# New instruction orders on five engines of an attention and recurrence block, with folded means and two transfer queues

## The reference

```python
def _ln(v, eps):
    return (v - mean(v, -1)) / sqrt(var(v, -1) + eps)

y = _ln(x, 1e-6)
q, k, v = (einsum('oc,ncij->noij', M, y) for M in (Wq, Wk, Wv))
qk = einsum('ncij,nchj->nihj', q, k) / d
qrq = einsum('ncij,chi->nihj', q, rq) / d
krk = einsum('ncij,chi->nihj', k, rk) / d
weight = softmax(qk + Gq * qrq + Gk * krk, axis=3)
out = einsum('nihj,nchj->ncij', weight, Gv1 * v) + einsum('nihj,chi->ncij', weight, Gv2 * rv)
x = x + out
t = x.reshape(16, 1024, 32)
Wx = einsum('bti,hi->bth', _ln(t, 1e-5), W)
Wx = (Wx - mean) * rsqrt(var + 1e-5) * gamma + beta      # over all b, t
y_t = sigmoid(Wx_t + y_(t-1) @ V.T)                      # 1024 steps
return t + ys
```

## Time and profile before

| | us |
|---|---|
| median of 3 runs | 154.19 |
| lowest, highest | 152.92, 155.33 |
| the profiled execution | 154.99 |
| its span, first to last instruction | 153.1 |

### The profile page before, as it was taken

The page is one execution under the profiler, slowest core; times in us unless marked ns, Lnnn a source line. Parts: engine busy times, 40 slices in busy tenths (PEclk is TensorE's granted clock), DMA queues, the critical chain, the costliest instruction groups (busy, mean ns, idle before and its releaser), DMA issues.

```text
span 153.1 us, 4782 instructions
## 1 busy us (share of the span) xinstructions
PE 101.6 (66%) x2063; PEld 70.5 (46%) x2064; DVE 96.2 (63%) x158; ACT 73.6 (48%) x161; POOL 61.9 (40%) x62
## 2 busy tenths in 40 slices
PE   0769978686598880999755950358208987999400
PEld 0313312475588770888655950112002336999400
DVE  5996874000304879705501896379988969888992
ACT  8957786347700236692230030332343449999500
POOL 8995439840000687740500054555343000003940
PEclk9999999999779999599999999557965999999965
DMA  4880899899000002434332000000000000000467
GB/s 138 294 206 0 189 206 237 192 226 188 12 4 4 4 4 54 106 75 101 91 90 58 4 4 0 2 0 0 0 0 0 4 0 0 0 6 0 144 197 208
DMA packets 9825, 11.67 MB, mean 76 GB/s; under 512 B 2828, under 2 KB 6924, under 8 KB 9804
## 3 DMA queue, kind: packets, MB, share of 16 engines
q1 hardware_dynamic: 9612, 10.84, 28.0%
q10 hardware_dynamic: 192, 0.52, 1.4%
HBM read 2.97 MB, written 2.10 MB: 33 GB/s over the span
## 4 chain that ended last, share of the span: by engine, by line
DVE 27%; PE 18%; SPq 15%; ACT 13%; issue 11%; DMA 8%; POOL 5%; POOLq 0%; ACTq 0%
SPq L286 7%; PE ps L1033 5%; PE ps L990 5%; ACT warm L658 4%; DMA gates<-in_L_conv_Gk_dram 4%; SPq L291 4%; DVE xin L351 3%; DMA v_tile<-u_tile 3%; PE ps L1043 3%; DVE stat L786 3%; DVE y_tile L357 3%; DVE u_tile L782 2%; DVE rel_tile L816 2%; PE ps L1020 2%; ACT v_tile L658 2%
## 5 line engine op out<-in xcount | busy, mean ns | idle before, releaser
L1054 PE MATMUL ps<-rel_tile,w_bd 128*128 128x512 f32 x16 | 12.6, 888 | 10.9 <-DVE rel_tile L816 10.9
L357 POOL TENSOR_TENSOR y_tile<-xin,u_tile 128x256 f32<-128x256 f32 (+1 forms) x7 | 7.1, 1049 | 23.6 <-DVE xin L351 23.6
L990 PE MATMUL ps<-spread,v_tile 128*32 128x64 f32 x512 | 13.5, 269 | 4.4 <-DMA v_tile<-u_tile 3.0
L407 POOL TENSOR_TENSOR att_tile<-att_tile,soft 128x1024 f32<-128x1024 f32 x4 | 7.8, 1946 | 19.1 <-DVE soft L746 19.1
L990 PEld LDWEIGHTS ps<-spread,v_tile 128*32 128x32 f32 x512 | 12.6, 195 | 5.4 <-issue 4.5
L757 DVE TENSOR_TENSOR u_tile<-ps,xin 128x512 f32<-128x512 f32 x8 | 5.5, 684 | 15.0 <-PE ps L1033 15.0
L596 ACT ACTIVATE square<-y_tile 128x512 f32<-128x512 f32 x8 | 4.9, 629 | 18.4 <-POOL y_tile L428 18.4
L428 POOL TENSOR_TENSOR y_tile<-u_tile,stat 128x512 f32<-128x512 f32 x7 | 7.3, 1048 | 15.6 <-DVE stat L788 15.6
L1043 PE MATMUL ps<-spread,v_tile 128*32 128x64 f32 x512 | 9.2, 223 | 6.4 <-issue 6.4
L887 DVE TENSOR_SCALAR ps<-att_tile,bnv 128x512 f32<-128x512 f32 (+1 forms) x18 | 12.3, 762 | 1.2 <-ACT warm L658 1.1
L1020 PE MATMUL ps<-w_bd,y_tile 128*32 128x128 f32 x256 | 9.2, 307 | 5.0 <-ACT v_tile L510 5.0
(11 more groups left out here) (103 smaller groups left out, 234.1 us busy)
## 6 DMA issues: line engine op xcount, KB each, us to landing
spread<-rel_tile SPq DMA_DIRECT2D x32, 64.0 KB, 2.0
out_dram<-y_tile SPq DMA_DIRECT2D x8, 256.0 KB, 2.3
xin<-in_x_dram SPq DMA_DIRECT2D x3, 512.0 KB, 4.9
spread<-att_tile SPq DMA_DIRECT2D x12, 128.0 KB, 3.5
v_tile<-u_tile SPq DMA_DIRECT2D x12, 128.0 KB, 3.1
xin<-in_x_dram SPq DMA_DIRECT2D x2, 256.0 KB, 2.8
spread<-u_tile SPq DMA_DIRECT2D x4, 128.0 KB, 2.3
att_tile<-in_L_conv_rv_dram SPq DMA_DIRECT2D x4, 128.0 KB, 2.7
```

Of the source, the lines that this page charges most:

```text
L357: return eng.tensor_tensor(result[:, :, rows, :], back[:, at:at + P * k].rearrange("p (q i j) -> p q i j", q=Q, i=k), x2[:, :, rows, :], A ...
L407: nc.gpsimd.tensor_tensor(att_m[:, n, :, :], att_m[:, n, :, :], soft[:, 0, n, :].unsqueeze(2).broadcast_to([P, C, C]), ALU.subtract).then_ ...
L990: return nc.tensor.matmul(ps[group(g), first + j // 8, at:at + Q * HALF].rearrange("p (q i) -> p q i", q=Q), u_by_q[:, g, :, j], y_bd[:, : ...
L1054: nc.tensor.matmul(bank(WX_BANK[k % 2]), w_bd[:, 1, :], by_row(tokens, k), start=True, stop=True).then_inc(S["wx_product"], 1)
```

## The change

It moves instructions in the lists of all engines, and does some of them in another way:

- VectorE's mean of a row is gone as an instruction. Where VectorE centres, the factor -1/32 is in the centring itself (`scalar_tensor_tensor` on the sums). Where GpSimd centres, it makes the mean itself with a small `tensor_scalar` ahead. This holds for both layer norms.
- SyncE loads rv behind `regroup_u(2)`.
- The add of `score_max` is a function of its own, `score_add`; the add of chunk 2 stands between the weight sums of chunks 0 and 1, that of chunk 3 behind the maximum of chunk 2.
- `weight_sum(3)` stands directly behind `weight_sum(2)`, and all eight `relv_out` behind it.
- TensorE computes all eight pieces of relative values ahead of the sums of half 0; the sums of half 1 follow those of half 0.
- ScalarE's value copies are spread between the exponentials and the turnings of the weights, and ScalarE issues the transfers of units 5 and 7 itself.
- In the second layer norm VectorE does residuals 0 to 3 in a row, then the sums of squares and reciprocals of these units, then two residuals ahead of the first transposes; ScalarE and GpSimd follow in corresponding orders (GpSimd centres four units before it scales the first).

```diff
@@ -169,12 +169,6 @@
         def side_bank(n):
             return bank(SIDE[n % 2])
 
-        def ln_centre(eng, n, done):
-            q, row, k = LN_PARTS[n]
-            eng.tensor_tensor(centred[:, q, row:row + k, :], xin[:, q, row:row + k, :],
-                              stat[:, 1, q, row:row + k].unsqueeze(2).broadcast_to([P, k, C]),
-                              ALU.subtract).then_inc(S[done], 1)
-
         def ln_scale(eng, n, done):
             q, row, k = LN_PARTS[n]
             eng.tensor_tensor(y[:, q, row:row + k, :], centred[:, q, row:row + k, :],
@@ -318,15 +312,15 @@
             spread_y(0)
             regroup_u(0)
             spread_y(1)
-            for g in range(G):
-                sp.dma_start(rv_in[group(g), :], rv.rearrange("c h i -> c (h i)")).then_inc(S["rv_in"], 16)
             regroup_u(1)
             spread_y(2)
             spread_y(3)
             regroup_u(2)
+            for g in range(G):
+                sp.dma_start(rv_in[group(g), :], rv.rearrange("c h i -> c (h i)")).then_inc(S["rv_in"], 16)
             for k, a in enumerate((gamma, beta)):
                 sp.dma_start(affine[:, k:k + 1], bass.AP(a.tensor, 0, [[0, G], [1, C], [1, 1]])).then_inc(S["affine_in"], 16)
-            for k in range(UNITS):
+            for k in (0, 1, 2, 3, 4, 6):
                 spread_att(k)
 
             for n, row, k in STORES:
@@ -365,11 +359,17 @@
             nc.gpsimd.memset(spread4[:, 2, :, :], 0.0).then_inc(S["spread_zero2"], 1)
             nc.gpsimd.memset(spread4[:, 3, 0:2, :], 0.0).then_inc(S["spread_zero3"], 1)
 
-            pool.wait_ge(S["ln_mean"], 3)
-            ln_centre(nc.gpsimd, 2, "ln_centred")
+            def ln_centre(n):
+                q = LN_PARTS[n][0]
+                pool.wait_ge(S["ln_sum"], n + 1)
+                nc.gpsimd.tensor_scalar(stat[:, 1, q, :], stat[:, 0, q, :], 1.0 / C, None, ALU.mult).then_inc(S["ln_mean"], 1)
+                pool.wait_ge(S["ln_mean"], q)
+                nc.gpsimd.tensor_tensor(centred[:, q, :, :], xin[:, q, :, :], stat[:, 1, q, :].unsqueeze(2).broadcast_to([P, C, C]),
+                                        ALU.subtract).then_inc(S["ln_centred"], 1)
+
+            ln_centre(2)
             nc.gpsimd.memset(spread4[:, 3, 2:4, :], 0.0).then_inc(S["spread_zero3"], 1)
-            pool.wait_ge(S["ln_mean"], 4)
-            ln_centre(nc.gpsimd, 3, "ln_centred")
+            ln_centre(3)
             pool.wait_ge(S["ln_rstd"], 3)
             pool.wait_ge(S["ln_squared"], 3)
             ln_scale(nc.gpsimd, 2, "y_ready_pool")
@@ -424,6 +424,8 @@
             weigh(3)
 
             def centre(k):
+                pool.wait_ge(S["t_sum"], k + 1)
+                nc.gpsimd.tensor_scalar(stat2[:, 1, k, :], stat2[:, 0, k, :], 1.0 / C, None, ALU.mult).then_inc(S["t_mean"], 1)
                 pool.wait_ge(S["t_mean"], k + 1)
                 nc.gpsimd.tensor_tensor(unit(x2n, k), unit(x2, k), stat2[:, 1, k, :].unsqueeze(2).broadcast_to([P, HALF, C]),
                                         ALU.subtract).then_inc(S["t_centred"], 1)
@@ -436,10 +438,10 @@
 
             centre(0)
             centre(1)
+            centre(2)
+            centre(3)
             scale(0)
-            centre(2)
             scale(1)
-            centre(3)
             scale(2)
             scale(3)
             centre(4)
@@ -568,22 +570,32 @@
             act.wait_ge(S["rv_in"], 16 * G)
             nc.scalar.mul(rv_s, rv_in.rearrange("p (h i) -> p i h", h=C), gates[:, 3:4]).then_inc(S["rv_scaled"], 1)
             nc.scalar.preload_act_table(ACT.Exp)
+            def spread_att(k):
+                half, q = k // Q, k % Q
+                act.wait_ge(S["weights_turned"], k + 1)
+                act.wait_ge(S["score_b_high"], 1)
+                for g in range(G):
+                    act.dma_start(spread4[group(q), q, g, BANK * half:BANK * (half + 1)], rel_tile[group(g), BANK * k:BANK * (k + 1)]
+                                  ).then_inc(S[f"att_in{half}"], 16)
+
             score_exp(0)
             score_exp(1)
-            turn_weights(0)
-            turn_weights(1)
             value_out(0)
             value_out(1)
-            score_exp(2)
+            turn_weights(0)
             value_out(2)
             value_out(3)
+            turn_weights(1)
+            value_out(4)
+            score_exp(2)
+            value_out(5)
+            value_out(6)
             score_exp(3)
-            value_out(4)
-            value_out(5)
+            value_out(7)
             turn_weights(2)
-            value_out(6)
-            value_out(7)
+            spread_att(5)
             turn_weights(3)
+            spread_att(7)
             nc.scalar.preload_act_table(ACT.Sqrt)
 
             def t_square(k):
@@ -614,16 +626,16 @@
             t_square(3)
             t_std(2)
             t_std(3)
+            t_square(4)
+            t_square(5)
+            t_std(4)
             wx_out(0)
+            t_std(5)
             wx_out(1)
-            t_square(4)
-            t_std(4)
+            t_square(6)
             wx_out(2)
-            t_square(5)
-            t_std(5)
+            t_square(7)
             wx_out(3)
-            t_square(6)
-            t_square(7)
             t_std(6)
             t_std(7)
             wx_out(4)
@@ -675,15 +687,19 @@
         def _(dve):
             nc.vector.memset(spread4[:, 0, 0:2, :], 0.0).then_inc(S["spread_zero0"], 1)
 
-            def ln_mean(n):
+            def ln_sum(n):
                 q, row, k = LN_PARTS[n]
                 rows = slice(row, row + k)
                 dve.wait_ge(S[f"x_in{n}"], 16)
                 nc.vector.tensor_reduce(stat[:, 0, q, rows], xin[:, q, rows, :], AX_X, ALU.add).then_inc(S["ln_sum"], 1)
+
+            def ln_centre(n):
+                q, row, k = LN_PARTS[n]
+                rows = slice(row, row + k)
                 dve.wait_ge(S["ln_sum"], n + 1)
-                dve.wait_ge(S["nought_set"], 1)
-                nc.vector.scalar_tensor_tensor(out=stat[:, 1, q, rows], in0=stat[:, 0, q, rows], scalar=1.0 / C,
-                                               in1=nought[:, 0:k], op0=ALU.mult, op1=ALU.add).then_inc(S["ln_mean"], 1)
+                nc.vector.scalar_tensor_tensor(out=centred[:, q, rows, :],
+                                               in0=stat[:, 0, q, rows].unsqueeze(2).broadcast_to([P, k, C]), scalar=-1.0 / C,
+                                               in1=xin[:, q, rows, :], op0=ALU.mult, op1=ALU.add).then_inc(S["ln_centred_dve"], 1)
 
             def ln_sum2(n):
                 q, row, k = LN_PARTS[n]
@@ -701,27 +717,24 @@
                 dve.wait_ge(S["ln_rstd"], n + 1)
                 ln_scale(nc.vector, n, "y_ready_dve")
 
-            ln_mean(0)
-            dve.wait_ge(S["ln_mean"], 1)
-            ln_centre(nc.vector, 0, "ln_centred_dve")
-            ln_mean(1)
-            dve.wait_ge(S["ln_mean"], 2)
-            ln_centre(nc.vector, 1, "ln_centred_dve")
-            ln_mean(2)
+            ln_sum(0)
+            ln_centre(0)
+            ln_sum(1)
+            ln_centre(1)
+            ln_sum(2)
             ln_sum2(0)
             ln_sum2(1)
             ln_rstd(0)
             ln_out(0)
             ln_rstd(1)
             ln_out(1)
-            ln_mean(3)
+            ln_sum(3)
             ln_sum2(2)
             ln_rstd(2)
             dve.wait_ge(S["w_in"], 16 * 3)
             nc.vector.transpose(wturned[:, :, :], wsmall[:, 0:3, :]).then_inc(S["turned"], 1)
-            ln_mean(4)
-            dve.wait_ge(S["ln_mean"], 5)
-            ln_centre(nc.vector, 4, "ln_centred_dve")
+            ln_sum(4)
+            ln_centre(4)
             ln_sum2(3)
             ln_rstd(3)
             ln_sum2(4)
@@ -730,7 +743,7 @@
             dve.wait_ge(S["rv_scaled"], 1)
             nc.vector.transpose(rv_t[:, :, :], rv_s).then_inc(S["rv_set"], 1)
 
-            def score_max(n):
+            def score_add(n):
                 first = SCORE_A if n < 2 else SCORE_B
                 if n < 2:
                     dve.wait_ge(S["score_a"], 1)
@@ -742,6 +755,8 @@
                 nc.vector.tensor_tensor(att[:, n, :, :, :],
                                         ps[:, first:first + 4, :].rearrange("p b (j q i) -> p q i (b j)", q=Q, i=HALF)[:, qs],
                                         rel_x[:, n, :, :, :], ALU.add).then_inc(S["score_sum"], 1)
+
+            def score_max(n):
                 dve.wait_ge(S["score_sum"], n + 1)
                 nc.vector.tensor_reduce(soft[:, 0, n, :], att_m[:, n, :, :], AX_X, ALU.max).then_inc(S["score_max"], 1)
 
@@ -757,22 +772,20 @@
                 nc.vector.tensor_tensor(x2[:, :, rows, :], side_bank(n).rearrange("p (i q j) -> p q i j", i=ROWS, q=Q),
                                         xin[:, :, rows, :], ALU.add).then_inc(S["relv_ready"], 1)
 
+            score_add(0)
             score_max(0)
+            score_add(1)
             score_max(1)
             weight_sum(0)
+            score_add(2)
```

(63 more changed lines are left out.)

## The result

The changed kernel takes 144.05 us (median of 4 runs, 143.42 to 144.52), beside 154.76 for the kernel before in the same group: ratio 0.938, 95% interval 0.928 to 0.948. Forecast were 141.4 us, with a range of 138.0 to 147.5. The profiled execution took 143.69 us with a span of 141.9, against 154.99 and 153.1.

The account below looks back on a forecast made before the run. Three stages with different limits: moving rows between partitions up to the scores, instruction order in the middle, then VectorE from first residual to last statistic. 154.99 - 2.5 - 4.55 - 6.55 = 141.4 us, range 138 to 147.5.

Parts of the forecast that it names:

- Part 2: Scores to first residual: the new order takes 34.15 us from the end of the first scores instead of 38.71, 4.55 gained.
- Part 3: First residual to last statistic: 29.5 us instead of 36.08, 6.55 gained by means off VectorE and shorter waits.
- part 1: Up to the scores: later rv loads bring 2.5 us, scores start at 37.6; folded means count nothing.
- the slower rival: Middle: relative_values(4), now ahead of all sums, waits for a late last weighing and shifts the residuals; slower overall; chance 0.03.
- Rival 3: First half's sums: crossings of sixteen KB of instructions are hidden, sums take 4.4 instead of 8.1, giving 137.7; chance 0.03.
- The floor of 27.6: First residual to last statistic: VectorE's busy time of 29.7 less 2.1 for eight means.
- the wait on GpSimd at unit 7: Second layer norm: VectorE's centring of unit 7 may wait for GpSimd; 0.6 us added.
- my lower bound of 1.2: Up to the scores: least gain in us expected from the later rv loads; upper bound 3.0.
- The second queue: Weight transfers partly issued by ScalarE: priced at 0, bounds 0 to +2.5; all 32 on SyncE would land at 78.1.
- Rival 1: Scores to sums: TensorE's instruction stream is the bound; lots of 4.4 us give 143.5, or 144.8; chance 0.18.
- Rival 2: Second layer norm: VectorE's new order brings no cover, only the fold; 5.3 us less gain, 146.7; chance 0.11.

Follow-up runs that it names:

- e5: Kernel before with only the middle's changes (score adds, softmax and value order, relative values ahead of sums, weight transfers by two engines): 150.78 us, ratio 0.979.
- e1: Kernel before with one edit, the rv loads issued behind regroup_u(2): 152.96 us, ratio 0.988.
- e4: Changed kernel with the second layer norm's means of units 0 to 6 made by VectorE again: 144.72 us, ratio 0.937.
- e10: Changed kernel with 16 instead of 4 blank matmuls behind the fourth projection of the second stage: 142.30 us, ratio 0.922.
- e6: Kernel before with only the second layer norm's changes (folded means, GpSimd's small means, new unit orders): 149.87 us, ratio 0.969.
- e2: Changed kernel with four instead of three full-size filler matmuls ahead of the first projection of u: 142.97 us, ratio 0.931.
- e7: Changed kernel with all eight units' weight transfers issued by SyncE again: 144.70 us, ratio 0.929.
- e8: Changed kernel with the second layer norm's means of units 0 to 6 made by ScalarE instead of GpSimd: 143.10 us, ratio 0.925.
- e11: Changed kernel with the edits of e2, e8 and e10 together: 141.62 us, ratio 0.916.
- e12: Changed kernel with the edits of e2, e8, e10 and e7 together: 142.97 us, ratio 0.925.
- e3: Changed kernel with the first layer norm's means of parts 2 and 3 made by VectorE again: 144.60 us, ratio 0.943.
- e9: Changed kernel run again, unedited, as base of a later group: 143.84 us, ratio 0.926.

## Why the prediction was right, and where it was off

The forecast of 141.4 is 2.3 us under the profiled execution. The terms of parts 2 and 3 are off by 0.4 and 0.8 us in opposite directions, which partly cancel; the rest is part 1.

**Part 2, the middle: right.** 4.99 us against 4.55, and e5 alone 4.90. The fifth relative value, the place of the slower rival, had its weights in time (weighed by 68.50; the row of pieces ran on behind that to 73.99, with one gap of 0.54 that waited for nothing the profile shows). The sums began 26.3 us behind the first add, 0.3 later than worked out, and the first residual came 7.4 us behind their start instead of 8.2, since their lots started every 3.5 us, under the 4.05 and 3.74 of the earlier trace rows. In the eight other profiles with this order and both queues the stage took 32.4 to 34.4 us, so it moves by a microsecond either way. Rival 3, hidden crossings, is out: gaps between lots of sums are in every run, mostly of 1.3 to 1.9 us (0.8 to 2.1). Only once did two lots run together at full pace, in e1 (250 matmuls in 4.12 us), behind relative values that had taken 5.36 instead of 3.95. The Trainium skill (Runtime: NRT & Kernel Launch, section Instruction fetch mechanics), which calls such a crossing mostly hidden, doesn't describe this row of matmuls, if these gaps are that.

**Part 3, the second layer norm: right, 0.8 us too much.** VectorE was the bound, as e4 shows by giving it its means back (32.85 us), but not the only one: with ScalarE's means the stage is 0.6 shorter than in e10 (29.31 against 29.90), though VectorE is busy 0.45 longer in it (28.34), because its waits for squares and roots fall from 1.3 to 0.2. So GpSimd's row, which the means lengthen, still held it up. The floor of 27.6 was 27.98. The idle time was 2.33, against 1.3 and 0.6. Of it 0.6 was for roots, 0.7 for squares and 0.5 for copies; the wait on GpSimd at unit 7, for which I had 0.6, didn't come (0.69 for the centring). GpSimd's mean was mis-sized, 0.254 us and 0.08 to hand over against 0.15, inside the bounds that I gave. TensorE's clock at the last four projections was missing altogether; e10 puts it at 0.4 to 1.1 us.

**Part 1, up to the scores: the term that failed.** I wrote that the transfers follow at the rate of the busy stretch, so that four fewer are 2.5 us, counted nothing for the folded means, and took 2.5 for scores at 37.6. Measured were scores at 39.39, 0.74 earlier than before, and 0.47 at the first add: less than my lower bound of 1.2. Three things stand in its place.

First, the price of the rv loads. Counted from the start of the first projection, so that the arrival of x drops out, scores begin 28.5, 28.6 and 27.3 us later in the profiles of before, e5 and e6 (rv early), and 26.3 to 27.4 in e2, e7, e8, e11 and e12 (rv late, all with projections of 1.92). The means are 28.1 and 26.7, so rv is worth 1.4 us at this mark, as well as groups of three and five profiles that just touch can say. I had priced its bytes at the rate of the whole stretch. Right behind the last transfer of u, where rv is alone but for a load of 0.5 KB, the changed kernel shows 311 GB/s at a DMA share of 0.86:

```profile
39.40:39.90 0.50, 0.50 (x21) 0.50 (x25) 0.00 (x0) 0.00 (x0) 0.00 (x0) 1.00 0.86 311
```

and e4 303 GB/s at 1.00. By these two rows the four loads of 128 KB keep the DMA engines busy for 1.4 to 1.7 us, an estimate, and not for the 2.5 of 208 GB/s.

Second, TensorE's clock. In the changed kernel the granted clock was 0.64 and 0.50 of full speed between 12 and 15 us, so partly at its lower level of 1.2 GHz, after 2.38 us without a matmul; before, it was 1.00 after 1.33 us. The projections took 3.50 instead of 1.92, and the u of group 1 came later. The windows from 24 to 26 us of the kernel before and of e2, to set beside the first row of the changed kernel's windows above:

```profile
24.00:26.00 2.00, 2.00 (x24) 0.43 (x16) 0.65 (x1) 1.69 (x3) 2.00 (x1) 1.00 0.97 256
```

```profile
24.00:26.00 2.00, 1.86 (x17) 0.44 (x19) 1.17 (x1) 1.69 (x2) 2.00 (x2) 1.00 0.92 209
```

The DMA share there was 0.97 and is 0.44, but with the projections at full clock, in e2, it is 0.92. So the hole isn't made by taking the loads away. SyncE's timeline in the changed kernel shows it waiting for u:

```profile
23.93 2.42 SPq L285 DMA_DIRECT2D v_tile<-u_tile  x4
26.44 6.20 SPq L280 DMA_DIRECT2D spread<-att_tile  x8
32.68 4.30 SPq L285 DMA_DIRECT2D v_tile<-u_tile  x4
37.03 1.98 SPq L320 DMA_DIRECT2D att_tile<-in_L_conv_rv_dram  x4
```

regroup_u(1) starts at 23.93, not 22.2, because its u was copied at 23.90. In all six late-rv profiles with projections of 3.2 to 3.5 (the changed kernel, e1, e3, e4, e9, e10) it starts at 23.4 to 23.9, and the DMA share from 24 to 26 us is 0.44 to 0.72; in the five with 1.92 it starts at 22.4 to 22.9, and the share is 0.90 to 0.93. What follows is held up in either: eight issues take 5.8 to 6.9 us and the next four 2.6 to 4.4, where four alone take 2.4 to 2.5. Part of that wait comes back: the count from the first projection to the scores is 27.3 to 28.1 in the six, mean 27.6, against 26.7. So of the 1.6 us that the projections lose, 0.8 arrive at the scores.

Third, the projections themselves start 0.47 us later, at 12.09. The experiments on the first layer norm put 0.16 of it down to the fold, and 0.31 to x, which came later in this execution.

Does the fold cost the clock? The idle time ahead of the projections grew by 1.05 us from the one profile to the other; the fold is 0.16 of that, x 0.31, and the earlier end of the filler matmuls (9.71 against 10.29) 0.58. With three filler matmuls the clock was lost in five of the seven profiles with the fold (e3 has only VectorE's part of it), and in one of the four without it (e1). With four it was kept in all three (e2, e11, e12). So the extra matmul is a cure as far as three profiles show, and the fold makes the loss likelier at most; that it is the cause isn't shown.

I had the rows for the second: the idle time ahead of the first projection stands in the trace of before. I read it as a wait that costs what it lasts. And I had followed the folded mean only to the y that SyncE moves, which waits for the gates, not to the y from which TensorE makes u. The Trainium skill (SBUF — State Buffer, section Who interferes with whom) says that a VectorE instruction with two SBUF inputs contends with a GpSimd instruction that reads SBUF, and that this contention is an exclusive lock. The traces agree: the scaling takes 0.69 us alone, 1.16 and 1.54 beside GpSimd's centring, and ends 0.56 and 0.54 behind it.

**The second queue: priced too low.** I put 32 issues on one queue at 0.6 us each. In e7 they took 25.59 us, 0.80 each, in e12 23.35. Their median is 0.59, but single ones take up to 1.6 and 1.7; what holds these the profile doesn't name. The trace of before had shown it:

```profile
58.24 24.02 SPq L299 DMA_DIRECT2D spread<-rel_tile  x32
```

By this row, 0.75 each, the last issue would end at 80.5, counted from 56.5 as in the prediction, instead of near 76. The sums' gaps of 5.10 and 1.18 us in e7 and e12 show that the last transfer there is the last to arrive, and that it decides only in some executions. With two queues no sum waits for a transfer in the eight profiles of the changed kernel and its variants, and in e5 one waits 0.2 us. The Trainium skill (DMA: Bandwidth & Descriptors, section Issuing engines are not separate DMA queues) says a second issuer saves issue time only, and that this is "usually small" beside the transfer. Here it was the larger part: the DMA engines were busy 0.34 of the time while SyncE issued alone in e7. So "usually small" is not for this case.

**Rival 1** (lots of 4.4 us) didn't come: in the changed kernel's profile the sums' lots start every 3.5 us, in e9 up to 4.0 and in e3 once 4.24 apart. The first lot of scores took 4.26 there. **Rival 2** is answered by the waits for reciprocals, 0.6 us.

What is open: why the first lot of scores is followed by 1.1 us of gap in some executions, by 0.35 to 0.8 in others and by hardly any in three (e3, e5, e8), and what makes executions of one kernel differ by 3.6 us (e9: 141.63 to 145.19). One part of it is a second loss of the clock ahead of the scores: in e8, e10 and e11 the granted clock was 0.50 from 33 to 36 us, and the last 160 matmuls of the relative scores took 6.0 to 6.3 us instead of 4.64; in e8 and e11 the scores start as soon as these end.

## What to carry to other kernels

Price a transfer that is taken out of a full stretch by what its own kind costs the DMA engines, not by the mean rate of the stretch, and look for the time at which the input of each later transfer is ready. Price a row of issues by a row of the same length in the trace, since single issues can be held up. When a step ahead of TensorE becomes longer or the filler ahead of it shorter, price the matmuls behind the gap at the low clock too, and fill the gap. An order in which an engine has two or more other units' work between a request and its answer, here sums of squares and roots, is worth the whole wait, and giving away small instructions from the bounding engine is worth more than their own length.

## What was not expected of the hardware

An idle time ahead of the first projections of 1.02 to 1.67 us kept the clock in all seven such profiles; 2.21, 2.38, 2.46 and 2.55 us lost it; 2.15 and 2.17 lost it and 2.16 kept it. A few tenths of a us, from the arrival of x or the length of the filler, so decide over 1.6 us at that place. Two issuing engines moved the 64 KB transfers at up to 208 GB/s, where SyncE alone moved them at 141 at most, though most issues of each took their usual 0.6 us. And a GpSimd instruction on 16 elements for each partition takes 0.25 us where VectorE's takes 0.17 alone.
